# Re-ordering the second layer of a two-layer transformer kernel: latents, downs and values in other places

## The chip, the cores and the metric

The kernel runs on one core of one Trainium2 chip. The metric is the device time of one execution in microseconds (us), lower is better. Beside the times stands one profiled execution, from which every row below is taken.

## The reference

Two layers run over 2048 tokens (8 sequences of 256) of width 256. The first adds a linear attention and a mixture of experts to the residual; the change doesn't touch it. The second layer is:

```
xn = layernorm(x)
c  = xn @ W_down + b                  # latents: 85 for q, 8 rotary, 128 for k and v
cn = layernorm(c per part) * g + b
q, k, v = cn @ W_up + b, rotary       # 16 heads of width 16
y  = softmax(q k^T / 4) v;  attn = y @ W_o + b_o
h  = gelu(xn @ Wg) * (xn @ Wu);  ffn = h @ Wd      # 4-bit weights, width 2048
out = x + attn + ffn
```

## The kernel before

Feature-major tiles of 512 tokens are used, so the second layer has four **groups** `g` of 512 tokens, each with two sequences `b0 = 2g` and `b1 = 2g + 1`. All products are in two or three parts of reduced precision (`prod`, lines 658 to 660: high by high, low by high, high by low), so each tile of 128 gate features is six matmuls of 512 columns.

Each engine runs its own list of steps, written out by hand in one Python loop per engine; semaphores tie them together. No scheduler moves anything: the order in the code is the order on the engine, and an instruction that waits holds all that stand behind it on its engine.

The feed-forward part is 16 tiles `t` of 128 features. Per tile:

- TensorE: `gate1(t)` into the bank `pm` (or `ring2` for t = 9 and 15), `up1(t)` into `pv`, later `down1(t)`, which adds into `acc`.
- ScalarE: `gelu(t)` reads the gate bank into `hf`; `hi(t)` rounds the product to `hh`.
- VectorE: `tile1(t)` multiplies by `pv` (line 2222).
- GpSimd: `split_h` makes the rest `hl` (line 1652).
- `gate1(t)` waits until `gelu(t - 1)` has read `pm`; `up1(t)` waits until `tile1(t - 1)` has read `pv`; `down1(t)` waits for `hl`.

The attention of a sequence is spread between these tiles:

- `latents` (TensorE), `bias_latents`, `latent_stats`, `latent_spread` and `norm_latents` (VectorE, with `latents_std` on ScalarE), `turn_latents` (transposes on TensorE), `affine_latents` (ScalarE, lines 1469 and 1473), `latents_lo` (VectorE).
- `up_q`, `up_k`, `up_v` (TensorE); `q_first`, `q_second`, `k_first`, `k_second` (ScalarE) and `q_rest`, `q_third`, `k_rest`, `k_third` (VectorE) split q and k into three parts `qp`, `kp`.
- SP copies the parts to slots in `qT` and `kT`: 24 transfers for a sequence (`place`, lines 617 and 621), 12 for heads 0 to 7, 12 for heads 8 to 15. The first three q transfers need `q_first`, the next three k transfers need `k_first`.
- `scores(b, j, ...)`: twelve banks of scores for the row maxima (`maxima` on VectorE); the first six use heads 0 to 7, so `scores(b, 6)` is the first that needs the last of the 24 transfers. `turn_max` and `place_max` put the maxima behind q.
- `probs(b, f, ...)`: scores again, turned; ScalarE takes exponentials (`probs_e`, line 1522), and ScalarE (`probs_hi`), VectorE (`probs_hi`, `probs_lo`) and GpSimd (`probs_lo`) split them. `values(b, hg)` (lines 1083, 1085) multiplies four heads by v for each head group `hg` of three banks; `normalize(b, hg)` on VectorE sums (`ys`, line 2301), inverts (`yr`) and scales. `values(b, hg)` waits until the sum of head group `hg - 1` has been taken, since both use `ring3`.

In groups 0 to 2 the routed rows of the next group are gathered and added (`weigh_first`, `weigh_rows`, `back`, `add_rows`), and the next group's layer norm is made (`ln_mean`, `ln_var`, `ln_std`, `ln_inverse`, `ln_wide`, `ln_scale`).

## Time and profile before

| What | Value |
|---|---|
| Median of 3 runs | 704.77 us |
| All runs | 701.17, 704.77, 705.35 us |
| The profiled execution | 707.44 us |
| Its span, first to last instruction | 705.6 us |
| Mean granted TensorE clock | 0.988 of full speed |
| TensorE matmul, busy | 661.8 us, 94% of the span |
| VectorE, ScalarE, GpSimd busy | 474.8, 384.1, 363.3 us |

The profiled execution took 1.84 us more than its span and 2.67 us more than the median of the runs. Busy time of TensorE is from modelled ends of pipelined matmuls: a matmul of 512 columns is shown with 0.39 us, while the next begins 0.23 us after it began. In a timeline the first number is the start, the second the duration, and the bracket at the end is the idle time before the instruction with what released it.

### The profile page before, as it was taken

Reading aid. Unit: us, or ns where it says so; the run is one execution under the profiler, and the core shown is the slowest. Engines: PE = TensorE matmul, PEld = TensorE weight load, DVE = VectorE, ACT = ScalarE, POOL = GpSimd, SP = SyncE. Lnnn points to the kernel's source line nnn. Section 1 sums busy time; section 2 is a strip of 40 time slices with the busy share of each in tenths; the row PEclk is TensorE's granted clock in tenths of the full one; section 3 lists DMA queues with packets and bytes.
Section 4 is the critical chain, followed back from the end, with each engine's and each line's share of the span. In section 5 each row is a group of like instructions: output and inputs, shape, how many; then the busy total and the mean of one; then the engine's idle time right before and its main releaser. Section 6 shows DMA issues by size and latency. Waiting matters only on the chain.

```text
span 705.6 us, 12735 instructions
## 1 busy us (share of the span) xinstructions
PE 661.8 (94%) x4396; PEld 530.6 (75%) x4396; DVE 474.8 (67%) x954; ACT 384.1 (54%) x691; POOL 363.3 (51%) x303
## 2 busy tenths in 40 slices
PE   7999999699969989999999899999999999999996
PEld 4777777688868977767778677778776777876774
DVE  6989877468646758685666677485868566567635
ACT  4654433256535665652955393675565295548273
POOL 3344668656655635373636275363637362426463
PEclk9999999899989999999999999999999999999999
DMA  8566846678865676130014121003303000302100
GB/s 306 180 203 220 288 164 212 221 266 264 278 198 183 216 269 196 70 92 2 1 46 131 34 51 42 1 2 112 98 2 91 1 1 31 79 13 65 27 2 31
DMA packets 66802, 82.72 MB, mean 117 GB/s; under 512 B 7090, under 2 KB 50354, under 8 KB 66738
## 3 DMA queue, kind: packets, MB, share of 16 engines
q1 hardware_dynamic: 63156, 73.39, 32.9%
q0 software_dynamic: 3072, 8.39, 3.7%
q8 instruction: 37, 0.61, 0.4%
q10 hardware_dynamic: 512, 0.13, 0.1%
q14 instruction: 25, 0.20, 0.1%
HBM read 40.34 MB, written 28.84 MB: 98 GB/s over the span
## 4 chain that ended last, share of the span: by engine, by line
PE 58%; DVE 12%; issue 11%; ACT 8%; SPq 5%; POOL 3%; DMA 2%; ACTq 0%; another core or an unknown queue 0%; POOLq 0%; DVEq 0%
PE acc L658 4%; PE acc L660 4%; PE acc L659 4%; PE ring L658 3%; SPq L621 3%; PE ring L660 3%; PE ring L659 3%; PE pv L658 3%; PE pm L658 3%; PE pm L660 3%; PE pm L659 2%; PE pv L660 2%; SPq L617 2%; PE pv L659 2%; PE ring L1028 2%
## 5 line engine op out<-in xcount | busy, mean ns | idle before, releaser
L1652 POOL TENSOR_TENSOR hl<-hf,hh 128x512 fp32r<-128x512 f32 (+1 forms) x76 | 103.2, 1360 | 203.7 <-ACT hh L1312 203.0
L1312 ACT ACTIVATE hh<-hf 128x512 fp32r<-128x512 f32 (+1 forms) x76 | 47.8, 632 | 80.5 <-DVE hf L2222 59.7
L658 PE MATMUL acc<-hh,wh 128*128 128x512 f32 (+1 forms) x168 | 71.9, 428 | 2.9 <-POOL hl L1652 2.9
L2286 DVE TENSOR_REDUCE mx<-ring 128x2 f32<-128x512 f32 (+1 forms) x96 | 61.6, 684 | 9.2 <-PE ring L1028 9.2
L660 PE MATMUL acc<-hl,wh 128*128 128x512 f32 (+1 forms) x168 | 66.6, 396 | 0.0
L659 PE MATMUL acc<-hh,wl 128*128 128x512 f32 (+1 forms) x168 | 66.3, 395 | 0.0
L2222 DVE TENSOR_TENSOR hf<-hf,pv 128x512 f32<-128x512 f32 x64 | 43.6, 681 | 25.0 <-PE pv L660 22.6
L1805 POOL TENSOR_TENSOR pl<-act,ph 128x512 f16<-128x512 f32 x32 | 43.2, 1361 | 23.3 <-ACT ph L1530 23.1
L658 PE MATMUL pv<-xh,wh 128*128 128x512 f32 x128 | 53.5, 418 | 0.0
L1504 ACT ACTIVATE hf<-pm 128x512 f32<-128x512 f32 x56 | 33.3, 595 | 36.0 <-PE pm L660 29.5
L660 PE MATMUL pv<-xl,wh 128*128 128x512 f32 x128 | 50.8, 397 | 0.0
L659 PE MATMUL pv<-xh,wl 128*128 128x512 f32 x128 | 50.5, 394 | 0.0
L658 PE MATMUL pm<-xh,wh 128*128 128x512 f32 (+1 forms) x116 | 49.6, 427 | 0.0
L660 PE MATMUL pm<-xl,wh 128*128 128x512 f32 (+1 forms) x116 | 46.0, 397 | 0.0
L659 PE MATMUL pm<-xh,wl 128*128 128x512 f32 (+1 forms) x116 | 45.8, 395 | 0.0
L1805 POOL TENSOR_TENSOR pl<-ex,ph 128x512 f16<-128x512 f32 x32 | 40.2, 1267 | 6.6 <-DVE ph L2315 6.6
L658 PEld LDWEIGHTS acc<-hh,wh 128*128 128x128 f32 (+1 forms) x168 | 31.8, 189 | 11.2 <-POOL hl L1652 5.8
L1022 PE MATMUL ring<-kT,qT 96*128 96x128 bf16 (+1 forms) x256 | 35.9, 247 | 4.1 <-DMA kT<-kp 3.6
L660 PEld LDWEIGHTS acc<-hl,wh 128*128 128x128 f32 (+1 forms) x168 | 31.6, 188 | 7.4
L1057 PE MATMUL ring<-qT,kT 98*128 98x256 bf16 (+1 forms) x256 | 36.4, 248 | 0.0
L2031 DVE TENSOR_TENSOR hf<-hf,ring 128x176 f32<-128x176 f32 x46 | 15.4, 334 | 30.3 <-ACT hf L1360 20.1
L659 PEld LDWEIGHTS acc<-hh,wl 128*128 128x128 f32 (+1 forms) x168 | 31.6, 188 | 5.3
(301 smaller groups left out, 2020.3 us busy)
## 6 DMA issues: line engine op xcount, KB each, us to landing
w4s<-w4hl SPq DMA_DIRECT2D x16, 512.0 KB, 3.9
ws<-qs SPq DMA_DIRECT2D x12, 512.0 KB, 5.1
qT<-qp SPq DMA_DIRECT2D x96, 64.0 KB
kT<-kp SPq DMA_DIRECT2D x96, 64.0 KB
xs<-yg SPq DMA_DIRECT2D x2, 2944.0 KB, 12.9
ys<-act SPq DMA_DIRECT2D x22, 256.0 KB
stage<-w SPq DMA_DIRECT2D x8, 608.0 KB, 5.3
xh<-xs SPq DMA_DIRECT2D x12, 256.0 KB
```

Of the source, the lines that this page charges most:

```text
L621: sp.dma_start(kT[i * DH:(i + 1) * DH, rows, :], kp[:, part, m, :]).then_inc(s_slot[m], 16)
L658: pe.matmul(o, w_hi, x_hi, start=first, stop=False, skip_group_check=True)
L659: pe.matmul(o, w_lo, x_hi, start=False, stop=False, skip_group_check=True)
L660: return pe.matmul(o, w_hi, x_lo, start=False, stop=last, skip_group_check=True)
L1022: pe.matmul(o, qT[0:SLOT, h, i * P:(i + 1) * P], kT[0:SLOT, h, 0:width], start=n == 0, stop=False, skip_group_check=True)
L1057: pe.matmul(o, kT[0:SLOT + 2, h, kt * P:(kt + 1) * P], qT[0:SLOT + 2, h, kt * P:SEQ], start=n == 0, stop=False, skip_group_check=True)
L1312: a.activation(h_parts(n)[0][0:rows, :], hf[0:rows, n % 2, :], ACT.Copy).then_inc(s_hh, 1)
L1504: a.activation(hf[:, n % 2, :], bank[:, :], ACT.Gelu_apprx_tanh).then_inc(s_act, 1)
L1652: return pool.tensor_tensor(dst, src, hi.bitcast(F32), ALU.subtract)
L1805: pool.tensor_tensor(pl[:, n % NP, :], exps(n), ph[:, n % NP, :], ALU.subtract).then_inc(s_plp, 1)
L2222: v.tensor_tensor(hf[:, n % 2, :], hf[:, n % 2, :], pv[:, :], ALU.mult).then_inc(s_h, 1)
L2286: v.tensor_reduce(mx[:, i, h0:h0 + nh], ring[j % 2][:, :].rearrange("p (n k) -> p n k", n=nh), AX.X, ALU.max).then_inc(s_mx, 1)
```

## The change

The change moves steps on four of the hand-written lists; SP's and GpSimd's own lists of work stay as they are, and no arithmetic differs. Its parts are:

1. `norm_latents(b0)` of the next group stands before the group's last residual sum on VectorE, and not behind it.
2. `turn_latents(b0)` stands behind `gate1(0)`, with `up_q`, `up_k`, `up_v` and the next `latents` each moved forward by one block; ScalarE and VectorE follow (`affine_latents` before `hi(0)`, `q_rest` and `q_third` before `tile1(1)`, and so on).
3. `down1(2)`, `down1(3)`, `down1(5)`, `down1(6)` and `down1(11)`, `down1(12)` stand one place later among the score and probability banks, and `up1(5)` and `gate1(6)` change places with `down1(4)` and with `turn_max` and `up_q(b1)`. On ScalarE `gelu(6)` stands behind `q_second(b1)`.
4. `gate1(9)` and `down1(7)` change places around `values(b0, 2)`, and so do `gate1(15)` and `down1(13)`. On VectorE `probs_hi` of the fourth head group stands before `normalize` of the second.
5. `ln_std` stands before `gelu(12)`, `ln_inverse` before `tile1(12)`, `ln_wide` before `gate1(13)`.


```diff
@@ -1148,48 +1148,47 @@
                     down(T0 * G + g * T1 + t, down_at(t), P, t == T1 - 1, t == 0)
 
                 gate1(0)
+                turn_latents(b0)
                 up1(0)
-                turn_latents(b0)
                 gate1(1)
+                up_q(b0)
                 up1(1)
-                up_q(b0)
                 down1(0)
+                up_k(b0)
                 gate1(2)
-                up_k(b0)
+                up_v(b0)
                 up1(2)
-                up_v(b0)
                 down1(1)
                 gate1(3)
+                latents(b1)
                 up1(3)
-                latents(b1)
-                down1(2)
 
                 if g < G - 1:
                     back(4 * g + 4)
                     back(4 * g + 5)
                 scores(b0, 0, 1)
+                down1(2)
+                scores(b0, 2, 3)
                 gate1(4)
-                scores(b0, 2, 3)
+                scores(b0, 4, 5)
                 up1(4)
-                scores(b0, 4, 5)
-                down1(3)
                 turn_latents(b1)
                 scores(b0, 6, 7)
                 if g < G - 1:
                     back(4 * g + 6)
                     back(4 * g + 7)
+                down1(3)
+                scores(b0, 8, 9)
                 gate1(5)
-                scores(b0, 8, 9)
+                scores(b0, 10, 11)
                 up1(5)
-                scores(b0, 10, 11)
+                if g < G - 1:
+                    pe.wait_ge(s_cadd, 4 * g + 8)
                 down1(4)
-                if g < G - 1:
-                    pe.wait_ge(s_cadd, 4 * g + 8)
-                gate1(6)
                 turn_max(b0)
                 up_q(b1)
+                gate1(6)
                 up1(6)
-                down1(5)
                 up_k(b1)
                 gate1(7)
 
@@ -1197,18 +1196,19 @@
                 up_v(b1)
                 up1(7)
                 probs(b0, 2, 3)
+                down1(5)
+                probs(b0, 4, 5)
                 down1(6)
-                probs(b0, 4, 5)
+                probs(b0, 6, 7)
                 gate1(8)
-                probs(b0, 6, 7)
                 values(b0, 0)
+                probs(b0, 8, 9)
                 up1(8)
-                probs(b0, 8, 9)
                 values(b0, 1)
                 probs(b0, 10, 11)
+                gate1(9)
+                values(b0, 2)
                 down1(7)
-                values(b0, 2)
-                gate1(9)
                 values(b0, 3)
                 up1(9)
 
@@ -1234,26 +1234,26 @@
                     ln_var(G + g + 1)
                 gate1(12)
                 up1(12)
+                if g < G - 1:
+                    ln_wide(G + g + 1)
                 gate1(13)
-                down1(11)
 
                 probs(b1, 0, 1)
                 up1(13)
-                if g < G - 1:
-                    ln_wide(G + g + 1)
                 probs(b1, 2, 3)
+                down1(11)
+                probs(b1, 4, 5)
                 down1(12)
-                probs(b1, 4, 5)
+                probs(b1, 6, 7)
                 gate1(14)
-                probs(b1, 6, 7)
                 values(b1, 0)
+                probs(b1, 8, 9)
                 up1(14)
-                probs(b1, 8, 9)
                 values(b1, 1)
                 probs(b1, 10, 11)
+                gate1(15)
+                values(b1, 2)
                 down1(13)
-                values(b1, 2)
-                gate1(15)
                 values(b1, 3)
                 up1(15)
                 down1(14)
@@ -1562,22 +1562,22 @@
                     a.wait_ge(s_w4, 4 * NQ)
                     a.activation(spread[:, :], spreadf[:, :], ACT.Copy).then_inc(s_spread, 1)
                 gelu(0)
+                affine_latents(b0)
                 hi(0)
-                affine_latents(b0)
                 gelu(1)
-                hi(1)
                 q_first(b0)
                 q_second(b0)
-                gelu(2)
+                hi(1)
                 k_first(b0)
                 k_second(b0)
+                gelu(2)
                 hi(2)
                 if g < G - 1:
                     weigh_first(4 * g + 4)
                 gelu(3)
+                if g < G - 1:
+                    weigh_first(4 * g + 5)
                 hi(3)
-                if g < G - 1:
-                    weigh_first(4 * g + 5)
 
                 latents_std(b1)
                 gelu(4)
@@ -1588,11 +1588,11 @@
                     weigh_first(4 * g + 7)
                 affine_latents(b1)
                 gelu(5)
+                place_max(b0)
                 hi(5)
-                place_max(b0)
-                gelu(6)
                 q_first(b1)
                 q_second(b1)
+                gelu(6)
                 hi(6)
                 k_first(b1)
                 gelu(7)
@@ -1623,11 +1623,11 @@
                 gelu(11)
                 place_max(b1)
                 hi(11)
+                if g < G - 1:
+                    ln_std(G + g + 1)
                 gelu(12)
                 hi(12)
                 gelu(13)
-                if g < G - 1:
-                    ln_std(G + g + 1)
 
                 probs_e(b1, 0, 1)
                 probs_hi(b1, 0)
@@ -2330,14 +2330,14 @@
                 tile1 = lambda t: gated1(T0 * G + g * T1 + t)
                 if g == 0:
                     turn_bias()
-                norm_latents(b0)
+                    norm_latents(b0)
                 tile1(0)
                 if g == 0:
                     v.wait_ge(s_w4, 4 * NQ)
                 latents_lo(b0)
-                tile1(1)
                 q_rest(b0)
                 q_third(b0)
+                tile1(1)
                 k_rest(b0)
                 k_third(b0)
                 tile1(2)
@@ -2345,10 +2345,10 @@
                 back0 = 4 * g + 4
                 if g < G - 1:
                     weigh_rows(back0)
+                bias_latents(b1)
+                if g < G - 1:
+                    weigh_rows(back0 + 1)
                 tile1(3)
-                if g < G - 1:
-                    weigh_rows(back0 + 1)
-                bias_latents(b1)
                 latent_stats(b1)
 
                 maxima(b0, 0, 1)
@@ -2358,10 +2358,10 @@
                     add_rows(back0 + 1)
                 maxima(b0, 2, 3)
                 norm_latents(b1)
-                tile1(4)
                 if g < G - 1:
                     weigh_rows(back0 + 2)
                 maxima(b0, 4, 5)
+                tile1(4)
                 if g < G - 1:
                     weigh_rows(back0 + 3)
                 maxima(b0, 6, 7)
@@ -2370,9 +2370,9 @@
                 if g < G - 1:
                     add_rows(back0 + 2)
                     add_rows(back0 + 3)
-                tile1(5)
                 maxima(b0, 10, 11)
                 split_max(b0)
+                tile1(5)
                 q_rest(b1)
                 tile1(6)
                 q_third(b1)
@@ -2390,8 +2390,8 @@
                 normalize(b0, 0)
                 probs_hi(b0, 2)
                 probs_lo(b0, 2)
+                probs_hi(b0, 3)
                 normalize(b0, 1)
-                probs_hi(b0, 3)
                 probs_lo(b0, 3)
                 normalize(b0, 2)
                 tile1(8)
@@ -2410,9 +2410,10 @@
                 maxima(b1, 8, 9, 10, 11)
                 split_max(b1)
                 tile1(11)
+                if g < G - 1:
+                    ln_inverse(G + g + 1)
                 tile1(12)
                 if g < G - 1:
-                    ln_inverse(G + g + 1)
                     ln_scale(G + g + 1)
 
                 probs_hi(b1, 0)
@@ -2423,8 +2424,8 @@
                 normalize(b1, 0)
                 probs_hi(b1, 2)
                 probs_lo(b1, 2)
+                probs_hi(b1, 3)
                 normalize(b1, 1)
-                probs_hi(b1, 3)
                 probs_lo(b1, 3)
                 normalize(b1, 2)
                 tile1(14)
@@ -2437,6 +2438,7 @@
                     bias_latents(b1 + 1)
                     latent_stats(b1 + 1)
                     latent_spread(b1 + 1)
+                    norm_latents(b1 + 1)
                 v.wait_ge(s_dn, T0 * G + T1 * (g + 1))
                 v.wait_ge(s_ao, b1 + 1)
                 for j in range(KD):
```

ScalarE in the second group, from the copy of the maxima (`mT`) to the exponentials' table. `hf<-pm` is a gelu, `hh<-hf` is `hi`, `qp` and `kp` are the splits of q and k for b1. Before:

```order
L1509 ACTIVATE mT<-ring 32x256 [waits max_turned]
L1512 DMA qT<-mT 1x16x256 [waits max_in]
L1512 DMA qT<-mT 1x16x256
L1504 ACTIVATE hf<-pm 128x512 [waits h_split,gate_ready]
L1483 ACTIVATE qp<-ring,bqc 128x256 [waits slots_in1,slots_in0,qkv]
L1483 ACTIVATE qp<-ring,bqc 128x256
L1488 ACTIVATE qp<-sq 128x512 [waits q_rest]
L1312 ACTIVATE hh<-hf 128x512 [waits h_used,gated]
L1493 ACTIVATE kp<-ring,gb 128x256 [waits qkv]
L1493 ACTIVATE kp<-ring,gb 128x256
L1504 ACTIVATE hf<-pm 128x512 [waits h_split,gate_ready]
L1522 ACT_TABLE_LOAD [waits probs_lo_by_dve,score_bank_turned]
```

After:

```order
L1509 ACTIVATE mT<-ring 32x256 [waits max_turned]
L1512 DMA qT<-mT 1x16x256 [waits max_in]
L1512 DMA qT<-mT 1x16x256
L1312 ACTIVATE hh<-hf 128x512 [waits h_used,gated]
L1483 ACTIVATE qp<-ring,bqc 128x256 [waits slots_in1,slots_in0,qkv]
L1483 ACTIVATE qp<-ring,bqc 128x256
L1488 ACTIVATE qp<-sq 128x512 [waits q_rest]
L1504 ACTIVATE hf<-pm 128x512 [waits h_split,gate_ready]
L1312 ACTIVATE hh<-hf 128x512 [waits h_used,gated]
L1493 ACTIVATE kp<-ring,gb 128x256 [waits qkv]
L1493 ACTIVATE kp<-ring,gb 128x256
L1504 ACTIVATE hf<-pm 128x512 [waits h_split,gate_ready]
```

The first `hf<-pm` here is `gelu(6)`. It stood right behind the two transfers; now `hi(5)` and the three q instructions, one of which waits for VectorE, stand before it. `gate1(7)` on TensorE waits for it in both kernels.

VectorE in the first group, third and fourth head groups of b0: `ph<-ex` is `probs_hi`, `pl` is `probs_lo`, and `ys`, `yr`, `std` are `normalize`. Before:

```order
L2320 TENSOR_TENSOR pl<-act,ph 128x512 [waits probs_hi_by_act]
L2301 TENSOR_REDUCE ys<-ring 128x136 [waits y_normed,y_bank]
L2303 RECIPROCAL yr<-ys 128x8 [waits y_steps]
L2305 TENSOR_TENSOR std<-ys,yr 128x2x64 [waits y_steps]
L2315 TENSOR_REDUCE ph<-ex 128x512 [waits y_bank,exponentials]
L2320 TENSOR_TENSOR pl<-ex,ph 128x512 [waits probs_hi_by_act]
L2301 TENSOR_REDUCE ys<-ring 128x136 [waits y_normed,y_bank]
L2303 RECIPROCAL yr<-ys 128x8 [waits y_steps]
L2305 TENSOR_TENSOR std<-ys,yr 128x2x64 [waits y_steps]
L2222 TENSOR_TENSOR hf<-hf,pv 128x512 [waits gate_up,activated]
```

After:

```order
L2320 TENSOR_TENSOR pl<-act,ph 128x512 [waits probs_hi_by_act]
L2315 TENSOR_REDUCE ph<-ex 128x512 [waits y_bank,exponentials]
L2301 TENSOR_REDUCE ys<-ring 128x136 [waits y_normed,y_bank]
L2303 RECIPROCAL yr<-ys 128x8 [waits y_steps]
L2305 TENSOR_TENSOR std<-ys,yr 128x2x64 [waits y_steps]
L2320 TENSOR_TENSOR pl<-ex,ph 128x512 [waits probs_hi_by_act]
L2301 TENSOR_REDUCE ys<-ring 128x136 [waits y_normed,y_bank]
L2303 RECIPROCAL yr<-ys 128x8 [waits y_steps]
L2305 TENSOR_TENSOR std<-ys,yr 128x2x64 [waits y_steps]
L2222 TENSOR_TENSOR hf<-hf,pv 128x512 [waits gate_up,activated]
```

`probs_hi` of the fourth head group (`ph<-ex`) has moved ahead of the whole `normalize` of the second head group.

ScalarE in the first group, from `hi(11)` to the exponentials of b1. Before:

```order
L1312 ACTIVATE hh<-hf 128x512 [waits h_used,gated]
L1504 ACTIVATE hf<-pm 128x512 [waits h_split,gate_ready]
L1312 ACTIVATE hh<-hf 128x512 [waits h_used,gated]
L1504 ACTIVATE hf<-pm 128x512 [waits h_split,gate_ready]
L1277 ACT_TABLE_LOAD
L1277 ACTIVATE lnc<-ring,epsb 128x4 [waits variance]
L1522 ACT_TABLE_LOAD [waits probs_lo_by_dve]
L1522 ACTIVATE act<-ring 128x512 [waits score_bank_turned]
```

After:

```order
L1312 ACTIVATE hh<-hf 128x512 [waits h_used,gated]
L1277 ACT_TABLE_LOAD
L1277 ACTIVATE lnc<-ring,epsb 128x4 [waits variance]
L1504 ACT_TABLE_LOAD [waits h_split]
L1504 ACTIVATE hf<-pm 128x512 [waits gate_ready]
L1312 ACTIVATE hh<-hf 128x512 [waits h_used,gated]
L1504 ACTIVATE hf<-pm 128x512 [waits h_split,gate_ready]
L1522 ACT_TABLE_LOAD [waits probs_lo_by_dve]
L1522 ACTIVATE act<-ring 128x512 [waits score_bank_turned]
```

`ln_std` (`lnc<-ring`) has moved ahead of `gelu(12)`, which now needs a table load of its own: three loads stand here where two stood.

## Rows read from the trace of the kernel before

**Rows 1.** The page, busy time of TensorE.

```profile
PE 661.8 (94%) x4396; PEld 530.6 (75%) x4396; DVE 474.8 (67%) x954; ACT 384.1 (54%) x691; POOL 363.3 (51%) x303
```

**Rows 2.** The chain in order of time: the layer norm's mean, `ln_mean`, in two groups.

```profile
323.33 0.88 PE ring L667 x2
...
438.10 0.88 PE ring L667 x2
```

**Rows 3.** Waits of TensorE from 300 us on: total, times, longest.

```profile
PE ring L1083 <- DVE yr L2303: 5.8, 8, 0.8
...
PE ring L1022 <- DMA kT<-kp: 3.6, 4, 1.9
...
PE acc L658 <- POOL hl L1652: 2.0, 5, 0.7
```

**Rows 4.** Timeline of the SP queue, second group, latents b0.

```profile
375.40 1.83 SPq L621 DMA_DIRECT2D kT<-kp  x3
...
389.62 0.60 SPq L621 DMA_DIRECT2D kT<-kp  x1
```

**Rows 5.** Timeline of TensorE, the waits in `scores(b0, 6)`, second and last group.

```profile
392.85 0.34 PE L1022 MATMUL ring<-kT,qT 96*128 96x128 bf16 x3 [1.87 <-DMA kT<-kp]
...
619.94 0.40 PE L1022 MATMUL ring<-kT,qT 96*128 96x128 bf16 x4 [0.29 <-DMA kT<-kp]
```

**Rows 6.** Timeline of ScalarE at the second group's start.

```profile
364.68 0.60 ACT L1504 ACTIVATE hf<-pm 128x512 f32<-128x512 f32 x1 [0.72 <-PE pm L660]
...
367.41 1.00 ACT L1469 ACTIVATE std<-ring,gb 93x256 f32<-93x256 f32 x2
...
368.31 0.71 ACT L1473 ACTIVATE cth<-std 93x256 fp32r<-93x256 f32 x2
...
370.85 0.82 ACT L1483 ACTIVATE qp<-ring,bqc 128x256 bf16<-128x256 f32 x2
...
372.61 0.63 ACT L1488 ACTIVATE qp<-sq 128x512 bf16<-128x512 f32 x1 [0.94 <-DVE sq L2253]
...
374.54 0.84 ACT L1493 ACTIVATE kp<-ring,gb 128x256 bf16<-128x256 f32 x2 [0.59 <-PE ring L660]
```

**Rows 7.** Timeline of TensorE, second group, `up1(6)` to `values(b0, 3)`.

```profile
402.25 0.40 PE L658 MATMUL pv<-xh,wh 128*128 128x512 f32 x1
...
403.66 0.39 PE L658 MATMUL acc<-hh,wh 128*128 128x512 f32 x1
...
406.24 0.39 PE L658 MATMUL pm<-xh,wh 128*128 128x512 f32 x1
...
410.43 0.40 PE L1057 MATMUL ring<-qT,kT 98*128 98x128 bf16 x4
...
425.13 0.18 PE L1083 MATMUL ring<-v,ph 128*128 128x51 bf16 x1 [0.72 <-DVE yr L2303]
```

**Rows 8.** Timeline of ScalarE, second group, from `place_max(b0)`.

```profile
401.96 1.17 ACTq L1512 DMA_DIRECT2D qT<-mT  x2
...
403.23 0.60 ACT L1504 ACTIVATE hf<-pm 128x512 f32<-128x512 f32 x1 [1.30 <-issue]
...
408.45 1.28 ACT L1522 ACT_TABLE_LOAD   x1
...
409.74 1.09 ACT L1522 ACTIVATE act<-ring 128x512 f32<-128x512 f32 x2
```

**Rows 9.** Timeline of VectorE, second group, third and fourth head groups.

```profile
421.45 0.57 DVE L2301 TENSOR_REDUCE ys<-ring 128x136 f32<-128x408 f32 x1
...
422.62 0.67 DVE L2315 TENSOR_REDUCE ph<-ex 128x512 f16<-128x512 f32 x1
...
424.99 0.67 DVE L2222 TENSOR_TENSOR hf<-hf,pv 128x512 f32<-128x512 f32 x1
```

**Rows 10.** Third group, `gelu(12)` on ScalarE, then `gate1(13)` on TensorE.

```profile
562.07 0.60 ACT L1504 ACTIVATE hf<-pm 128x512 f32<-128x512 f32 x1 [1.57 <-PE pm L660]
...
563.27 0.39 PE L658 MATMUL pm<-xh,wh 128*128 128x512 f32 x1
```

More of the change, by code:

```diff
@@ L1180, in _ @@
                     back(4 * g + 7)
+                down1(3)
+                scores(b0, 8, 9)
                 gate1(5)
-                scores(b0, 8, 9)
+                scores(b0, 10, 11)
                 up1(5)
-                scores(b0, 10, 11)
-                down1(4)
                 if g < G - 1:
                     pe.wait_ge(s_cadd, 4 * g + 8)
-                gate1(6)
+                down1(4)
                 turn_max(b0)
                 up_q(b1)
+                gate1(6)
                 up1(6)
-                down1(5)
                 up_k(b1)
@@ L2347, in _ @@
                     weigh_rows(back0)
-                tile1(3)
+                bias_latents(b1)
                 if g < G - 1:
                     weigh_rows(back0 + 1)
-                bias_latents(b1)
+                tile1(3)
                 latent_stats(b1)
```

2 lines of the change are left out of this document (1 added, 1 removed).

## The prediction

> **What bounds the kernel now.** I read the busy times first, then the chain, then TensorE's waits. TensorE is busy for 661.8 us of the span [rows 1], and in the second layer its share is higher still: what is left to gain there is the sum of its waits. The chain gives the length of a group as the distance from one `ln_mean` to the next: 438.10 - 323.33 = 114.8 us [rows 2]. Four groups follow each other, and a term of 0.5 us in each is worth 2 us. The list of waits shows where TensorE stands still [rows 3]: before `values`, 5.8 us in 8 waits put down to VectorE's normalising; before score banks, 3.6 us in 4 waits for the last copy into `kT`; before downs, 2.0 us in 5 waits for `hl`. Each is shown some 0.16 us too short, because the modelled end of a matmul (0.40 us after its start) lies behind the start of the next (some 0.23). So at most some 14 us, 2% of the time, can be had by any order at all, and a new order can bring new waits. I went through the second group (g = 1) engine by engine: with the start that each instruction would have after its last wait, and durations from its row.
>
> **Part 1 and 2, the group's start.** The last copy binds. In the second group the k copies begin at 375.40, when `k_first` is done, and the last is issued at 389.62 [rows 4]; `scores(b0, 6)` begins at 392.85 after 1.87 us of waiting, which is 17.5 us after `k_first` [rows 5]. SP's list is the same in both kernels, so that distance stays, and what counts is when `k_first` ends. Before: gelu(0) at 364.68, affine at 367.41 (1.00 and 0.71 us), q_first at 370.85, q_second done at 373.24, k_first done at 375.38 [rows 6]. After: the transposes stand behind `gate1(0)` and are done when gelu(0) is (365.3); affine ends at about 366.8; `latents_lo` waits for `tile1(0)` ahead of it on VectorE and ends at 367.95, so `up_q` begins 1.5 us earlier. q_first then ends at 369.85, and q_first to q_second takes 2.39 us as before. But now `q_third` (0.7), `tile1(1)` (0.7) and `hi(1)` (0.63) stand one behind the other ahead of `k_first`, which ends at about 374.2: 1.15 us earlier, not 1.5. Against this, `down1(3)` no longer stands ahead of `scores(b0, 6)`. It is six matmuls, 403.66 - 402.25 = 1.41 us [rows 7], and now has to be done after the last copy has landed, when before it filled part of the wait. Net 1.41 - 1.15 = **+0.25 us** in the second to fourth group (the wait is there in the last one too [rows 5]); in the first, where the copies land in time, I take -0.1. The bounds: -0.5 if TensorE's own place decides, +1.4 if `k_first` gains nothing. Moving `norm_latents` ahead costs nothing: the residual sum is first needed by `down1(0)`, several us later.
>
> **Part 3, gelu(6).** `place_max` ends its two transfers on ScalarE at 403.13, and gelu(6) follows at 403.23 [rows 8]; `gate1(7)`, which overwrites the bank that it reads, begins at 406.24 [rows 7], 2.4 us after gelu(6) is done. That slack is the cover, and the change takes it: `hi(5)` (0.63), then q_first to q_second (2.39, as in the second group's start [rows 6]) stand ahead. On the clock of before, gelu(6) would run from about 406.15 to 406.75, and gate1(7) would start near 406.85: **+0.6 us** per group. Behind it, `tile1(6)` and `hi(6)` come after `q_second`, then k_first, gelu(7), and the table load of 1.28 us [rows 8]; the first exponential would begin near 410.75 where it was at 409.74, and `probs(b0, 2)`, at 410.43 before [rows 7], needs it done. With gate1(7) late as well TensorE asks at about 411.05 and gets it at 411.4: **+0.35 us**. Bounds for the two together: 0 (if q_first begins before hi(5) is through its wait) and 1.4 (if the transfers on ScalarE's queue take longer).
>
> **Part 3 and 4, the probabilities.** From `probs(b0, 2)` to `values(b0, 3)` TensorE needs 425.13 - 410.43 = 14.7 us [rows 7]. In it lie five blocks of six matmuls (7.4, with the slower first matmul behind a score bank), five pairs of probability banks and three head groups of values (some 5.3, an estimate from the pair of 0.7 us that stands at 410.43). That leaves about 2.0 us of waits, and the largest is the last, 0.72 us shown at 425.13 [rows 7]. The chain of exponentials, splits and sums sets this pace. After, `down1(5)` (1.41) is put into the same stretch. Its time is no new work, it is taken from ahead of `up_k`; it fills the waits: **-2.0 us**. What comes back: a wait of 0.3 for exponentials and 0.2 at `values(b0, 2)`, because the sum `ys` of the second head group (0.57 at 421.45) now stands behind `probs_hi` of the fourth (0.67 at 422.62) [rows 9], which waits for an exponential: **+0.5**. Then everything that VectorE does from there to `tile1(8)` (424.99) is one chain of two normalisings, a split and the product, and `up1(9)` waits for `tile1(8)`: **+0.5**.
>
> Sum for b0: 0.25 + 0.6 + 0.35 - 2.0 + 0.5 + 0.5 = **+0.2 us** per group, and 4 x 0.2 = 0.8 us.
>
> **Part 3 to 5 for b1.** `down1(11)` moves in the same way and fills the waits before `values`. But the probabilities now start right behind `gate1(13)`: `probs(b1, 2)` asks before the first exponential is done, since the table load ahead of it takes its 1.28 us, and waits some 0.6 us. At the end the VectorE chain from the eleventh exponential to `tile1(14)` is as long as before, and `up1(15)` and then `down1(14)` wait for it. I follow both orders to `up1(15)` and get the same time within 0.2 us: **0**. `ln_std` ahead of gelu(12) brings one more table load in each of three groups. gelu(12) ended at 562.67 in the third group, `gate1(13)` began at 563.27 [rows 10]. After, Sqrt's load runs while ScalarE would be idle; then come the root (0.3) and Gelu's load (1.28), and gelu(12) ends at about 564.0; `ln_wide`, 0.9 us, now stands ahead of `gate1(13)` and covers it: gate1(13) would ask at 564.15. The cover is 0.15 us thin; without it the price is up to 1.3 us in each of three groups. The row shows the load from 408.45 to 409.73 and the exponential at 409.74, so nothing follows a load [rows 8]. The Trainium skill says otherwise ("ScalarE: Activation LUTs", What ACT_TABLE_LOAD costs): about 1283 ns for the load and about 1380 ns of drain, some 2.66 us for a switch. The trace agrees with the first figure and shows no second one behind it; by the page the two switches would make gelu(12) 2.8 us later, and the sum 8 us higher.
>
> **The forecast.** The changed program would take 0.8 us more than the profiled execution's 707.44, so 708.2 there; the runs' median lies 2.67 lower, which gives 705.6 us. That is no change: a measurement of this kernel can tell about 1% (7 us) from none.
>
> **The rivals.**
> *The waits go and nothing takes their place.* The waits before `values` and for the copy vanish (5.8 + 3.6 us [rows 3]) and most of those for `hl`. For it: these are the waits that the moves aim at, and -2.0 of my sum is of this kind. Against: it needs gelu(6) to be in time and the VectorE chain before `up1(9)` to be short. It would give 704.8 - 9.4 = 695.4; half of it, 700. Chance 0.15 for gains of more than 3 us.
> *gelu(6) decides.* The late bank delays `gate1(7)`, the exponentials start later by as much, and since these set the pace to `values(b0, 3)` the down that was moved in fills nothing. It decides if the first exponential comes over 1.5 us later than now, relative to `turn_max`; I have 1.0. Then b0 costs 0.25 + 0.6 + 0.9 + 0.5 us, and with the 0.6 at `probs(b1, 2)` unrecovered 2.85 per group: 704.8 + 11.4 = 716. In half measure 710. Chance 0.15 for losses of more than 4 us.
> *The third table load.* ScalarE stands idle behind each load for as long as the load takes (1.28), gelu(12) comes 2.6 us later, `gate1(13)` waits 2.4 us in three groups: 704.8 + 0.8 + 7.2 = 712.8. Chance 0.03, as the row shows no such gap. This is what the page of the Trainium skill would have.
> *The forecast*, within 3 or 4 us: 0.67.
>
> **How the numbers follow.** Within 1% are 697.7 to 711.8. Of the first rival a third lies below, of the second a third above, and most of the third. Faster 0.07, same 0.83, slower 0.10. The range holds the forecast with its bounds (-0.75 and +1.15 per group in the first term, a us either way for gelu(6)), the nearer half of the two rivals, and the spread of the three runs (701.2 to 705.4): 700.0 to 710.5.
>
> **What would show it.** In the changed kernel's trace: `scores(b0, 6)` still waits for `kT`, longer than before; a new wait of TensorE on ScalarE's gelu at `gate1(7)`, 0.4 to 0.8 us, four times; the waits before `values` much shorter; a wait before `up1(9)` or `up1(15)` on VectorE; 3 more table loads with no wait at `gate1(13)`; a group of 114.6 to 115.2 us. The forecast is wrong if the group's length moves by over 1.7 us, most likely because the probability stretch doesn't take in its down, or gelu(6) costs nothing.

## The result, and the profile after

The changed kernel takes 719.53 us (median of four runs, 718.25 to 721.34) beside 705.06 us for the kernel before on the same chip (four runs, 701.17 to 708.48). The ratio is 1.020 with a 95% interval of 1.016 to 1.024: slower by 14 us. The forecast was 705.6 us, in a range to 710.5. The profiled execution took 720.65 us, with a span of 718.8 (before 705.6).

The busy times of the page of the profile, after, beside [rows 1]:

```profile
PE 665.9 (93%) x4396; PEld 530.6 (74%) x4396; DVE 486.2 (68%) x954; ACT 388.6 (54%) x694; POOL 361.5 (50%) x303
```

TensorE has the same 4396 matmuls and is busy 4 us longer, while the span grew by 13: most of the loss is waiting. The chain in order of time, after, at the three `ln_mean`:

```profile
326.08 0.88 PE ring L667 x2
...
445.21 0.88 PE ring L667 x2
...
562.80 0.88 PE ring L667 x2
```

They are 119.1 and 117.6 us apart where [rows 2] has 114.8. Both traces reach the second layer at the same time (`gate1(0)` of the first group at 249.63 after, 249.68 before), so all of the 13.2 us lies in the four groups. TensorE's waits from 300 us on, after (total, times, longest), to be laid beside [rows 3]:

```profile
PE ring L1083 <- DVE ys L2301: 5.9, 16, 0.4
PE ring L1022 <- DMA kT<-kp: 3.1, 5, 1.4
PE pv L658 <- DVE hf L2222: 2.4, 8, 0.3
PE acc L658 <- POOL hl L1652: 2.1, 5, 0.6
PE ring L1057 <- ACT act L1522: 2.0, 4, 0.5
PE ring L706 <- DVE ex L2043: 1.7, 2, 1.2
PE pm L658 <- ACT hf L1504: 1.4, 4, 0.5
PE ring L706 <- DVE act L2043: 0.4, 1, 0.4
```

None of the old waits is gone. Before `values` there are 5.9 us in 16 places now. Before, it was 5.8 in 8 places [rows 3] and these seven smaller ones, 7.2 in all:

```profile
PE ring L1083 <- DVE ys L2301: 1.4, 7, 0.2
```

Five kinds are new: before `up1(9)` and `up1(15)` (`pv`), before the third bank of probabilities (L1057), before `gate1(7)` (`pm`), and two before `back` (L706). The second group's timeline of TensorE, after, shows one of each kind in its place (of the two before `back` only one; L1057 stands in b1):

```profile
395.57 0.40 PE L1022 MATMUL ring<-kT,qT 96*128 96x128 bf16 x4 [1.42 <-DMA kT<-kp]
...
397.34 0.49 PE L706 MATMUL ring<-identf,ex 128*128 128x128 f32 x2 [0.49 <-DVE ex L2043]
...
411.69 0.50 PE L658 MATMUL pm<-xh,wh 128*128 128x512 f32 x1 [0.28 <-ACT hf L1504]
...
429.16 0.18 PE L1083 MATMUL ring<-v,ph 128*128 128x51 bf16 x1 [0.41 <-DVE ys L2301]
...
431.75 0.18 PE L1083 MATMUL ring<-v,ph 128*128 128x51 bf16 x1 [0.33 <-DVE ys L2301]
...
432.82 0.50 PE L658 MATMUL pv<-xh,wh 128*128 128x512 f32 x1 [0.30 <-DVE hf L2222]
...
460.95 0.40 PE L1057 MATMUL ring<-qT,kT 98*128 98x128 bf16 x4 [0.51 <-ACT act L1522]
```

To find where the time came in, I take each group's length (first matmul of `gate1(0)` to first matmul of `down1(15)`) and two points between, `up1(6)` and `up1(9)`. After less before, in us:

| stretch | group 1 | group 2 | group 3 | group 4 | sum |
|---|---|---|---|---|---|
| to `up1(6)` | +2.10 | +2.01 | +1.44 | +0.11 | 5.7 |
| `up1(6)` to `up1(9)` | +0.65 | +0.66 | +0.70 | +0.68 | 2.7 |
| `up1(9)` to `down1(15)` | +1.72 | +0.92 | +0.97 | +1.28 | 4.9 |
| group | +4.47 | +3.59 | +3.11 | +2.07 | 13.2 |

The first line tells that something happens in the three groups that have a `back` and not in the last; the other two come in all four. Two views say what. The first is ScalarE's idle time in the second layer by line, after (busy, mean | idle before, and by whom):

```profile
L1530 ACT ACTIVATE ph<-act 128x512 f16<-128x512 f32 x32 | 20.2, 631 | 4.8 <-PE ring L1085 4.6
L1530 ACT ACTIVATE ph<-ex 128x512 f16<-128x512 f32 x32 | 20.0, 640 | 3.3 <-PE ring L1085 2.9
```

`probs_hi` on ScalarE waits 7.5 us for `values` (L1085). Before, the same two kinds of rows are

```profile
L1530 ACT ACTIVATE ph<-ex 128x512 f16<-128x512 f32 x32 | 19.9, 637 | 0.3
L1530 ACT ACTIVATE ph<-act 128x512 f16<-128x512 f32 x32 | 19.3, 631 | 0.3
```

The split probabilities lie in `NP` = 6 slots (`NP = 6`, and `s_y >= (n - NP) // 3 + 1` ahead of the write), so `probs_hi` of bank 6 needs `values(b, 0)` done, and that of bank 9 needs `values(b, 1)`. In ScalarE's timeline of the second group, after, these are the two waits between the load of Exp's table and that of Gelu's:

```profile
414.26 1.28 ACT L1522 ACT_TABLE_LOAD   x1
...
423.87 0.63 ACT L1530 ACTIVATE ph<-ex 128x512 f16<-128x512 f32 x1 [0.23 <-PE ring L1085]
...
426.68 0.63 ACT L1530 ACTIVATE ph<-act 128x512 f16<-128x512 f32 x1 [0.47 <-PE ring L1085]
...
428.21 0.60 ACT L1522 ACTIVATE ex<-ring 128x512 f32<-128x512 f32 x1 [0.41 <-POOL pl L1805]
...
429.48 1.28 ACT L1504 ACT_TABLE_LOAD   x1
```

Load to load is 429.48 - 414.26 = 15.22 us. Before, it is 14.11 in the same place (408.45 in [rows 8], the next load at 422.56). Counted from the load, the exponential behind the second wait begins 0.62 us later than before (at 427.22, so 12.96 us for 12.34), and the last one 1.1 us later, after a wait of 0.41 put down to GpSimd's `probs_lo`. What delays `values` is seen on TensorE: `values(b0, 0)` begins 8.73 us behind the load (422.99), where before it was 7.31 (415.76), later by one down of 1.41.

The second view is the wait before `back`. In the first group it is 1.81 us as the profile puts it down (1.97 from the gap between the matmuls), and the trace's rows for the source line of `weigh_rows` on VectorE (x1: min/median/max ns) are

```profile
L2043 DVE SCALAR_TENSOR_TENSOR ex<-ex,share x1: 477/477/477, 275.1 to 275.1; 128x256 f32<-128x256 f32 x1
L2043 DVE SCALAR_TENSOR_TENSOR act<-act,share x1: 1189/1189/1189, 278.5 to 278.5; 128x256 f32<-128x256 f32 x1
its engine sat idle before it (us, times) until:
  ACT act L1377: 1.1, 1
```

The product for the fourth row tile starts late, because `weigh_first` on ScalarE (L1377) stands behind `hi(4)`, which waits for `tile1(4)`, which now stands behind `maxima(b0, 4, 5)`. And it takes 1.19 us where the other takes 0.48: GpSimd works at `hl` beside it,

```profile
278.12 1.26 POOL L1652 TENSOR_TENSOR hl<-hf,hh 128x512 fp32r<-128x512 f32 x1 [4.09 <-ACT hh L1312]
```

### The profile page after: what moved, and what is told of

Same layout as the page of the kernel before. It is cut to its first block, busy times and chain, and to the rows that moved or that the text cites. A ratio compares the mean times of both kernels' runs of the same rounds, so it can differ in the third digit from the quotient of the medians.

```text
span 718.8 us, 12738 instructions
## 1 busy us (share of the span) xinstructions
PE 665.9 (93%) x4396; PEld 530.6 (74%) x4396; DVE 486.2 (68%) x954; ACT 388.6 (54%) x694; POOL 361.5 (50%) x303
## 4 chain that ended last, share of the span: by engine, by line
PE 54%; DVE 14%; issue 12%; ACT 8%; POOL 4%; SPq 3%; DMA 3%; ACTq 1%; another core or an unknown queue 1%; POOLq 0%; DVEq 0%
PE acc L658 4%; PE acc L660 4%; PE acc L659 4%; PE ring L1028 3%; PE ring L658 2%; PE ring L1057 2%; PE ring L660 2%; PE ring L659 2%; PE pv L658 2%; PE pv L660 2%; PE pv L659 2%; POOL hl L1652 2%; PE ring L1022 2%; PE pm L658 2%; PE pm L660 2%
## 5 line engine op out<-in xcount | busy, mean ns | idle before, releaser
L658 PE MATMUL acc<-hh,wh 128*128 128x512 f32 (+1 forms) x168 | 73.6, 438 | 3.0 <-POOL hl L1652 3.0
L1805 POOL TENSOR_TENSOR pl<-act,ph 128x512 f16<-128x512 f32 x32 | 40.5, 1278 | 17.8 <-ACT ph L1530 17.8
L1057 PE MATMUL ring<-qT,kT 98*128 98x256 bf16 (+1 forms) x256 | 35.9, 247 | 2.3 <-ACT act L1522 2.0
```

What stands on the lines that cost most here:

```text
L658: pe.matmul(o, w_hi, x_hi, start=first, stop=False, skip_group_check=True)
L1057: pe.matmul(o, kT[0:SLOT + 2, h, kt * P:(kt + 1) * P], qT[0:SLOT + 2, h, kt * P:SEQ], start=n == 0, stop=False, skip_group_check=True)
L1805: pool.tensor_tensor(pl[:, n % NP, :], exps(n), ph[:, n % NP, :], ALU.subtract).then_inc(s_plp, 1)
```

## The experiments

Each kernel ran against the kernel before on the same chip; the chips differ (before: 706.04 us in the first four runs, 697.05 in the next four, 696.91 in the next three, 708.46 in the last), so only ratios are compared. Beside the ratio stands what the trace gives: the lengths of the four groups less those of the kernel before. In two stretches each profile is followed to a hundredth: from the load of Exp's table to `up1(9)` in b0, and from that load to Gelu's on ScalarE.

| kernel | ratio (95%) | groups, us | sum | load to `up1(9)` | load to load |
|---|---|---|---|---|---|
| before | | | | 17.29 | 14.11 |
| after | 1.020 (1.016, 1.024) | +4.5 +3.6 +3.1 +2.1 | +13.2 | 18.56 | 15.22 |
| a_down3 | 1.010 (1.007, 1.014) | +3.2 +0.5 +2.3 +1.7 | +7.6 | 18.55 | 15.22 |
| a_wfirst | 1.010 (1.007, 1.012) | +2.2 +1.2 +1.6 +2.0 | +7.0 | 18.55 | 15.22 |
| a_late | 1.006 (1.003, 1.008) | +2.1 -0.4 +2.8 +0.1 | +4.6 | 17.70 | 14.11 |
| a_gelu6 | 1.015 (1.011, 1.018) | +3.6 +1.4 +2.2 +1.4 | +8.6 | 18.55 | 15.22 |
| a_norm | 1.015 (1.012, 1.018) | +4.2 +1.5 +3.6 +1.8 | +11.0 | 18.40 | 15.22 |
| b_start | 0.992 (0.988, 0.995) | +0.1 -1.4 -1.7 -0.6 | -3.6 | 17.29 | 14.11 |
| b_start2 | 0.994 (0.992, 0.996) | +0.0 -1.9 -1.6 -0.7 | -4.2 | | |
| b_late | 0.998 (0.996, 1.001) | +1.5 -0.5 +0.3 -0.5 | +0.7 | 17.47 | 14.10 |
| b_ph3 | 1.005 (1.002, 1.007) | +0.8 +0.2 +1.2 +0.9 | +3.0 | 17.67 | 14.10 |
| b_best | 0.993 (0.991, 0.996) | +0.7 -1.4 -1.3 -1.2 | -3.2 | 17.50 | 14.12 |
| c_four | 0.992 (0.990, 0.995) | +0.2 -1.3 -1.6 -1.2 | -3.9 | 17.47 | 14.10 |
| d_all | 0.990 (0.985, 0.994) | -0.5 -2.7 -2.6 -1.8 | -7.5 | 17.46 | 14.11 |

A profile is one execution. Five of these groups hold a stretch at half clock (the granted clock is 0.5 there), each worth up to 1.7 us: the second of the changed kernel, the third of a_late, the first of b_late, b_best and c_four. So a group is good to about 1.5 us, and the last group, which has none, to 0.1.

**The waits before back, from TensorE's side: a_down3.** `down1(3)` stands again where it covered the chain.

```diff
                 up1(4)
+                down1(3)
                 turn_latents(b1)
...
                     back(4 * g + 7)
-                down1(3)
-                scores(b0, 8, 9)
                 gate1(5)
-                scores(b0, 10, 11)
+                scores(b0, 8, 9)
                 up1(5)
+                scores(b0, 10, 11)
```

> The changed kernel with down1(3) put back ahead of turn_latents(b1), and gate1(5) and up1(5) one place earlier behind it, as before the change. Theory R (rows back): in groups 0 to 2 the second pair of back() waits for weigh_rows of the last routed rows, which on VectorE and ScalarE stands behind tile1(4) and hi(4); before, down1(3) lay ahead of it and covered it. With down1(3) ahead again the time at which back() may run does not change, so the 1.41 us of the down is saved in each group: about 5.5 us, near 714. The rival, that the scores region costs nothing and the probability region all of it, leaves the saving at what the copy into kT binds, 1.2 us in each of four groups too, so this run tells by the trace: R wants the start of the back() transposes, counted from gate1(0), unchanged at 29.5 to 30.1 us, and the next gate1(5) 1.4 us earlier; if the kT copy alone bound, back() would follow scores(b0, 7) without a wait.

It came out as expected: the second `back` of the first group still begins 30.08 us after `gate1(0)`. `up1(6)` comes 1.2 us earlier there than in the changed kernel, and the wait before `back` falls from 1.8 to 0.7. The down fills the wait for the keys as well: those waits, 3.1 us in the changed kernel, are 1.1 here. Over the four groups the stretch to `up1(6)` goes from +5.7 to -0.3 us. The late product itself still takes 1.20 us.

**The same waits, from ScalarE's side: a_wfirst.**

```diff
                     weigh_first(4 * g + 6)
-                hi(4)
                 if g < G - 1:
                     weigh_first(4 * g + 7)
+                hi(4)
```

> The changed kernel with one step moved on ScalarE: weigh_first of the last routed rows stands ahead of hi(4), not behind it. Theory R: hi(4) waits for tile1(4), which now comes late, and the rows wait behind it. In the first group, where the rows have long landed, the wait of TensorE before back() (1.8 us) goes; in the third (1.24 us) most of it; in the second, where the landing binds, it stays. About 3 us less than the changed kernel, near 716.5. If the landing of the gathered rows binds everywhere, nothing changes.

It gained more than expected: the stretch to `up1(6)` goes from +5.7 to -0.15 us in four groups. The trace's row for the same line, in this kernel:

```profile
L2043 DVE SCALAR_TENSOR_TENSOR act<-act,share x1: 477/477/477, 273.1 to 273.1; 128x256 f32<-128x256 f32 x1
```

With its operand there in time, the product runs before GpSimd begins and takes 0.48 us. No wait of TensorE before `back` is left, in the second group neither, where I had put it down to the landing of the rows; and the half-clock stretch that the changed kernel has behind this wait (below) is missing: that is a part which I had not counted.

**The slots: a_late.** One down fewer stands ahead of the values; it comes behind the last bank of probabilities instead.

```diff
                 down1(5)
                 probs(b0, 4, 5)
-                down1(6)
-                probs(b0, 6, 7)
                 gate1(8)
+                probs(b0, 6, 7)
                 values(b0, 0)
-                probs(b0, 8, 9)
                 up1(8)
+                probs(b0, 8, 9)
                 values(b0, 1)
                 probs(b0, 10, 11)
+                down1(6)
                 gate1(9)
                 values(b0, 2)
                 down1(7)
```

and the same with `down1(12)` for b1.

> The changed kernel with one down moved within each probability stretch: down1(6) from ahead of probs(b0, 6) to behind probs(b0, 11), and down1(12) likewise in b1. Theory S (slots): the ninth bank's rounding on ScalarE must wait until values(b, 1) has read its slot, so the chain to values(b, 2), values(b, 3) and up1(9) starts at values(b, 1), which the extra down ahead of it delays. With the down behind it, values(b, 1) comes 1.4 us earlier, the waits before values(b, 2) and (b, 3) (0.57 and 0.50 us) and up1(9) (0.46) go: 1 to 1.4 us in each of eight halves, 8 to 11 us, near 710. Theory E, that of the prediction: the first exponential sets the pace, so it does not matter where in the stretch the down stands, within 1 us of the changed kernel, 719.

This decides between the two: of the 14 us, 10 come back by the ratios and 8.6 by the traces (the first is good to some 3.5 us, the second holds a half-clock stretch on both sides). `gate1(8)` and `up1(8)`, `gate1(14)` and `up1(14)` go back by one pair of banks as well, but what stands ahead of `values(b, 0)` and `values(b, 1)` differs by the down alone, and `values(b0, 0)` begins 7.32 us behind the load again. ScalarE's idle rows of a_late are those of before again,

```profile
L1530 ACT ACTIVATE ph<-ex 128x512 f16<-128x512 f32 x32 | 19.9, 638 | 0.3
L1530 ACT ACTIVATE ph<-act 128x512 f16<-128x512 f32 x32 | 19.3, 632 | 0.3
```

the loads stand 14.11 us apart (407.75 and 421.86 in the second group), the stretch to `up1(9)` is 0.86 us shorter and that to `up1(15)` 1.17 (18.28 to 17.11): 4 x (0.86 + 1.17) = 8.1 us. The waits before `values` are gone from the list altogether.

**gelu(6): a_gelu6.**

```diff
                 hi(5)
+                gelu(6)
                 q_first(b1)
                 q_second(b1)
-                gelu(6)
```

> The changed kernel with gelu(6) on ScalarE ahead of q_first(b1) again, behind hi(5). The wait of TensorE at gate1(7) (0.53 us, four times) should go, and the exponentials of b0 start some 0.5 us earlier, so that the 0.3 us at probs(b0, 2) goes too. 0.5 to 0.9 us per group: 2 to 3.5 us less than the changed kernel, near 716.5. If the late gate is made up for in the waits behind it, 719.

As expected. The four waits at `gate1(7)` are gone, and Exp's table load follows `up1(6)` by 4.93 us where the changed kernel has 5.60 (before 6.20): 0.67 us in each group.

**VectorE's swap: b_ph3 (alone, on the kernel before) and a_norm (undone, in the changed kernel).**

```diff
                 probs_lo(b0, 2)
-                normalize(b0, 1)
                 probs_hi(b0, 3)
+                normalize(b0, 1)
```

> The kernel before with one part of the change alone: on VectorE probs_hi of the fourth head group ahead of normalize of the second, in both halves. values(b, 2) waits 0.7 us longer for its sum, values(b, 3) 0.8 us less for its split, up1(9) and up1(15) come at the end of the same VectorE chain: within 1 us of before.

> The changed kernel with one pair of VectorE's steps turned back in both halves of a group: the sum and division of the second head group again ahead of the high part of the fourth. Nothing else is undone. In the kernel before, that swap alone made each half 0.4 us longer (a ratio of 1.005). If the order of these two steps sets the pace in the changed kernel as well, this kernel gains 0.4 us in each of 8 halves, 3.2 us: a ratio of 1.0155 to before, where the changed kernel has 1.02. If instead the pace of the changed kernel's probability stretch is set by the places for probabilities that come free late, the swap is covered and the ratio stays at 1.02, with waits of about 1 us before the third and fourth values together in either order.

Alone the swap costs 0.38 us in each half, 3.0 us in all, which is more than I had put on it. TensorE's waits of b_ph3 from 300 us on:

```profile
PE ring L1083 <- DVE ys L2301: 5.7, 7, 0.8
PE ring L1022 <- DMA kT<-kp: 2.8, 3, 1.5
PE pv L658 <- DVE hf L2222: 2.3, 8, 0.3
```

The eight waits before `up1(9)` and `up1(15)` (`pv`) come with the swap. In the changed kernel undoing it gives back only 0.16 and 0.14 us per half by the trace, 1.2 us, and the waits before `up1(9)` stay: there the slots bring them as well, and the swap is mostly covered. With the slots repaired it is worth little more (0.22 and 0.16, c_four against a_late below), so the slots alone are not its cover; what else is was not tried. The ratio of a_norm is lower by 0.005, but it and the changed kernel ran on different chips and their intervals overlap, so 4 us for the swap are not shown.

**The start alone: b_start, and again on another chip as b_start2.** The kernel before with the change's moves up to `latents(b1)` on TensorE, up to `latents_std(b1)` on ScalarE and up to `maxima(b0, 0, 1)` on VectorE, and `norm_latents` ahead of the sum: parts 1 and 2 of the change.

```diff
                 gate1(0)
-                up1(0)
                 turn_latents(b0)
+                up1(0)
                 gate1(1)
-                up1(1)
                 up_q(b0)
+                up1(1)
```

> The kernel before with the first parts of the change alone: norm_latents(b0) ahead of the residual sum, turn_latents, up_q, up_k, up_v and latents(b1) a block earlier, with ScalarE and VectorE following, up to latents(b1). k_first ends 1.15 to 1.3 us earlier, and the copy into kT lands as much earlier; down1(3) still stands ahead of scores(b0, 6). So the waits for kT shrink by that: 1.2 us in the second and third group, 0.4 in the last, nothing in the first: 2.8 us less than before, near 702. If these parts cost something by themselves (the theory that the loss of the change lies at the group's start), it is slower than before.

> The kernel before with only the group's start re-ordered, the same program that gave 0.9918 on another chip, beside the two others here. If its gain is the earlier copies of the keys, as its trace had it (0.1, 1.4, 1.7 and 0.65 us in the four groups, 3.8 us), the ratio is 0.992 to 0.996 again. If the gain on the other chip was a matter of where the clock fell, it comes out between 0.996 and 1.002 here.

Both are faster than before, by 0.8 and 0.6%. No wait for `kT` is left in TensorE's list of b_start over the whole second layer:

```profile
PE ring L1083 <- DVE yr L2303: 5.6, 8, 0.7
PE acc L658 <- POOL hl L1652: 2.1, 5, 0.7
PE ring L1083 <- DVE ys L2301: 1.4, 7, 0.2
```

**The late downs alone: b_late.** The kernel before with its downs 5 to 7 and 11 to 13 placed as in a_late.

> The kernel before with the probability stretches re-ordered so that one more down stands in them, but behind values(b, 1): down1(5) from ahead of up_k(b1) to behind probs(b0, 3), down1(6) to behind probs(b0, 11) with gate1(9) and down1(7) as in the change, and the same for 11, 12, 13 in b1. Theory S: the waits before values(b, 2) and (b, 3), 0.4 and 0.9 us, go; a wait of some 1.3 us for the first exponential comes before probs(b, 2), since TensorE gets there 1.4 us earlier. About 0.5 us saved in each half: 4 us less than before, near 701. Theory E gives the same here. If both are wrong and the stretch takes no down in, 1.4 us per half is lost: 716.

Only 1 us came, within the interval of none. TensorE's waits in the whole second layer tell why:

```profile
PE ring L1057 <- ACT act L1522: 5.5, 8, 1.1
```

All waits before `values` (5.8 us [rows 3], and 1.4 in seven smaller ones put down to `ys`) are gone, and 5.5 us of waits for exponentials stand in their place. `down1(5)` no longer stands ahead of the probabilities, so TensorE comes to them 1.4 us earlier, but ScalarE's first exponential comes only 0.5 us earlier.

**Both on the kernel before: b_best.**

> b_start and b_late together. Their waits lie apart, so the two savings add: 2.8 and 4 us, near 698. If the down moved out from ahead of up_k(b1) brings a new wait at gate1(7), less.

Nothing over b_start, for the same reason.

**The repairs together: c_four.** The changed kernel with a_wfirst, a_late, a_gelu6 and a_norm.

> The changed kernel with four repairs together: the weighing of the fourth row tile on ScalarE ahead of the high part of tile 4; the second of the two downs that were put between the probabilities a few banks later (down1(6) behind probs(b0, 11), down1(12) behind probs(b1, 11)); gelu(6) ahead of the queries of the next half; the division of the second head group ahead of the fourth's high part. If the four causes are separate, the single runs add up: against before a group is some 1.2 to 1.8 us shorter, 5.8 us in four groups, a ratio of 0.991 to 0.992, because what is left of the change (the earlier start and one down that fills) is a gain. If they hide one another, so that a repair beyond the second finds nothing left to give, the ratio stays at 1.00 or above.

The ratio is the one forecast for separate causes: 0.992, where the changed kernel has 1.020. Its four groups sum to -3.9 rather than -5.8; 1.1 of that is a half-clock stretch in its first group. Beside the earlier start, what it has over b_late is that `turn_max(b0)` stands ahead of `gate1(6)`, and Exp's load follows `up1(6)` by 4.93 us where b_late has 5.71: TensorE then waits less for the first exponential. That this one move is the cause was not tried alone. Its waits from 300 us on have one large entry left:

```profile
PE ring L1022 <- DMA kT<-kp: 3.9, 4, 2.3
PE ring L1057 <- ACT act L1522: 2.0, 4, 0.5
PE acc L658 <- POOL hl L1652: 1.8, 5, 0.7
```

**And the start's order of before between up1(3) and down1(4): d_all.** c_four with, among others,

```diff
                 scores(b0, 4, 5)
+                down1(3)
                 turn_latents(b1)
```

> Everything that earned something, in one kernel: the four repairs of the changed kernel, and between up1(3) and down1(4) TensorE's order of before again, with down1(3) ahead of turn_latents(b1) and tile1(4) ahead of maxima(b0, 4, 5) on VectorE. The start's gain as the traces of the kernel with the start alone show it (0.1, 1.4 to 1.9, 1.7 and 0.65 us in the four groups) and what the kernel with four repairs gains from up1(6) on (1.1, 1.6, 1.5 and 1.3 us) lie in different stretches. If they add up, that is 9.4 us: a ratio of 0.986 to 0.988, faster than either kernel before it. If an earlier start only makes the probabilities wait longer for the exponentials, the ratio is that of the better of the two, 0.992.

0.990 (0.985, 0.994), 8 us below the kernel before: the best point estimate of all, though its interval overlaps those of c_four and the start alone, which ran on other chips. By the traces it is 7.5 us of the 9.4 that I had added up. The wait for the keys, from 300 us on, is down to one:

```profile
PE ring L1057 <- ACT act L1522: 2.3, 5, 0.5
PE acc L658 <- POOL hl L1652: 1.8, 5, 0.7
PE ring L1022 <- DMA kT<-kp: 0.7, 1, 0.7
```

## Why the prediction was wrong

The forecast was +0.2 us per group; the last group, which has neither `back` nor a half-clock stretch, has +2.07, and the others +3.1 to +4.5. By its own steps:

**The group's start** (forecast +0.25, -0.1 in the first): right in size. The last group has +0.11 at `up1(6)`, and the other three, less their waits before `back` and the half-clock stretch of the second, have +0.13, -0.3 and +0.04. The wait for `kT` stays, but it didn't grow as I said: 3.1 us where it was 3.6.

**The second pair of back** (not in the sum): missed. I priced `down1(3)`'s move only against the last copy of the keys. It also covered `weigh_first`, `weigh_rows` and the transposes of `back` behind them, and the change made that chain later as well: `tile1(4)` moved behind `maxima(b0, 4, 5)`, and `hi(4)` and `weigh_first` on ScalarE wait for it. By the gaps between matmuls it cost 1.97, 0.65 and 1.40 us in three groups (4.0), and in the second group a half-clock stretch behind it (some 1.7). a_down3 and a_wfirst each give nearly all of it back, from two sides.

**gelu(6)** (+0.6, bounds for it and the exponential together 0 to 1.4): right. `gate1(7)` waits 0.44 to 0.53 us in each group, and undoing it alone gives 0.67. **The first exponential** (+0.35): right, +0.33 at the third bank of probabilities. From `turn_max(b0)` to Exp's load it is 8.03 us where it was 7.22, 0.8 later; the forecast had 1.0, and the rival wanted over 1.5. The rival "gelu(6) decides" came nearest to the measured time, but gelu(6) carries only 0.67 us of a group.

**The fill** (-2.0): this is the step that failed. I took the 2.0 us of waits between `probs(b0, 2)` and `values(b0, 3)` as room for `down1(5)`, and wrote myself that "the chain of exponentials, splits and sums sets this pace". Even so a block of 1.41 us can fill at most 1.41, so the term was too large by 0.6 in its own sum. And where a chain sets the pace, a block put among its links fills nothing unless it leaves the links where they are. `down1(5)` and `down1(6)` both stand ahead of `values(b0, 0)`, one down more than before; `values` comes later, the six slots come free later, ScalarE waits (7.5 us in the layer), its last exponential is 1.1 us later, and TensorE waits before the last values again (0.57 and 0.50 us by the gaps, before 0.40 and 0.87). From the table load to `up1(9)` the program takes 18.56 us instead of 17.29 (+1.27). Only the load itself comes 0.60 us earlier behind `up1(6)` (6.20 to 5.60). The sum of this stretch is +0.67, where my terms gave -0.05. The slots are nowhere in the prediction, though the wait is written in the code.

**The wait before up1(9)** (+0.5): right in size (0.46 us, eight times). The swap on VectorE alone brings it (b_ph3), and so do the slots (it is there in a_norm, gone in a_late). **The sum behind the split** (0.2 at `values(b0, 2)`) was 0.57 with the other causes on top.

**b1** (0 +- 0.2): wrong, +0.9 to +1.7, by the same step. The 0.6 us at `probs(b1, 2)` was right (0.68, four times), and so was the wait before `up1(15)`; that the stretch would swallow both was not. a_late takes 1.17 us of it away. **ln_std** was right: no wait at `gate1(13)` in the third group. In ScalarE's timeline, after,

```profile
570.73 1.28 ACT L1277 ACT_TABLE_LOAD   x1
572.02 0.26 ACT L1277 ACTIVATE lnc<-ring,epsb 128x4 f32<-128x4 f32 x1
572.30 1.28 ACT L1504 ACT_TABLE_LOAD   x1
573.60 0.60 ACT L1504 ACTIVATE hf<-pm 128x512 f32<-128x512 f32 x1
```

gelu(12) ends at 574.20 and `gate1(13)` starts at 574.29, with nothing put down to a wait. Each function follows its load at once. The Trainium skill ("ScalarE: Activation LUTs", What ACT_TABLE_LOAD costs) adds about 1380 ns of drain to a load; in these rows there is none, and the rival of the third table load, which waits behind each load, is out. Only in the first group did `gate1(13)` wait 0.83 us.

**The waits go** (the first rival, 695.4 us): they didn't; the kernel is slower. c_four and d_all (0.992 and 0.990) show that re-ordering had 5 to 7 us in it, but not in the order that the change has.

What stays open: the traces account for 13.2 us of the 14.5 between the medians, and by their sums the single repairs overlap (each of them also lost the half-clock stretch of the second group). How the 8 us of the slots part exactly between the wait for `values(b, 0)` and that for `values(b, 1)` was not tried; a kernel with more slots would show it, and no run has one.

## What to carry to other kernels

A wait before a step can be filled only if the filler does not stand ahead of anything that the waited-for chain itself needs: follow the chain round through its buffers, for a ring of slots closes it into a loop in which the consumer paces the producer. When a block is taken away from a place, ask for every chain that it covered there, not only for the one at which the change aims. And of a change of many parts, test the parts alone: here the first two were a gain of 0.6 to 0.8%, hidden under four moves that cost 2.8%.

## What the runs showed of the hardware

A multiply-add of `weigh_rows` on VectorE (128x256, two tensors from SBUF) took 0.48 us alone and 1.19 to 1.20 us when GpSimd's 1.26 us subtraction ran beside it; a chain that is late by a few tenths can so be late by 0.7 more. The Trainium skill ("SBUF — State Buffer", SBUF: two separate sides) says that the two engines share a port pair as an exclusive lock, held for a whole instruction; the trace agrees in kind, and whether the multiply-add waited for all of the other it can't show.

The clock fell to half in the middle of the second layer in the changed kernel, right behind two waits of 1.59 and 0.65 us that stand within 2 us of each other. Stretches of the timeline of after (busy times, granted clock, DMA share, GB/s):

```profile
394.00:397.00 3.00, 1.43 (x14) 0.84 (x12) 1.60 (x3) 1.78 (x4) 1.27 (x1) 1.00 0.28 70
397.00:402.00 5.00, 4.66 (x18) 3.41 (x19) 3.05 (x7) 0.88 (x3) 0.00 (x0) 0.66 0.00 0
402.00:406.00 4.00, 4.00 (x22) 3.02 (x20) 3.39 (x8) 0.60 (x1) 0.00 (x0) 1.00 0.00 0
```

0.66 of the full clock over 5 us is 1.7 us lost, almost as much as the waits themselves. In a_late the same happens in the third group behind 1.16 and 1.06 us. It is no rule of these runs: in the third group of the changed kernel 0.84 and 1.40 us stand as close together without it, and single waits of up to 2.50 us (c_four) had none. The first layer has one to three such stretches in every trace, and their number differs between executions of like programs; that is why the span of one profile is compared here group by group and not as a whole.
